# First attention of a fused two-layer kernel: values computed once per pair of token tiles, keys stored by even and odd chunk

## What is computed

```
x = x + attention(layernorm(x))          # 4 sequences of 1024 tokens, 256 features
qkv = xn @ W_qkv                         # 256 -> 3 x (16 heads x 16)
allowed = (j <= i) & (j > i - 64)        # each query sees itself and 63 tokens before it
out = softmax(q k^T / 4 + mask) v        # per head
return out @ W_out
```

## Time and profile before

| | |
|---|---|
| median of 3 runs | 2348.84 us |
| the profiled execution's own time | 2363.76 us |
| its span in the profile | 2362.0 us, mean granted clock 0.906 |
| first attention | 0 to about 460.8 us |
| matmuls of the values (L551), first attention | 384 |

### The profile page before, as it was taken

One profiled execution on the slowest core, in us unless ns is written; L12 is line 12 of the kernel. 1 busy time (PEld: TensorE's weight loads), 2 busy tenths in 40 slices (PEclk: granted clock), 3 DMA queues, 4 the chain that ended last, 5 costly groups with the idle time before them and its releaser, 6 DMA issues. The chain is left out here.

```text
span 2362.0 us, 49456 instructions
## 1 busy us (share of the span) xinstructions
PE 2011.9 (85%) x18325; PEld 1356.7 (57%) x18325; DVE 1704.1 (72%) x2695; ACT 1213.4 (51%) x2196; POOL 474.0 (20%) x610
## 2 busy tenths in 40 slices
PE   5889888799979999989978899999999999971270
PEld 4667666468879999978867333343343343330150
DVE  5666666566658888856644789999999999647822
ACT  4455454343256666632233278888888888530010
POOL 1010001010022322224343112112212211300054
PEclk9899999799989999999989589999999999675585
DMA  2000000191043333333268886854864701020054
GB/s 90 2 0 0 0 0 0 60 342 62 28 157 124 120 111 120 107 100 113 89 206 281 105 73 59 73 38 43 67 41 44 62 20 37 19 72 0 27 159 136
DMA packets 222809, 188.18 MB, mean 80 GB/s; under 512 B 121533, under 2 KB 201369, under 8 KB 220505
## 3 DMA queue, kind: packets, MB, share of 16 engines
q1 hardware_dynamic: 202872, 146.71, 30.9%
q0 software_dynamic: 18080, 27.17, 4.3%
q10 hardware_dynamic: 1728, 12.58, 1.5%
HBM read 121.37 MB, written 64.75 MB: 79 GB/s over the span
## 5 line engine op out<-in xcount | busy, mean ns | idle before, releaser
L2029 ACT ACTIVATE ga_probT<-banks 128x512 f32<-128x512 f32 x1024 | 556.7, 597 | 172.7 <-PE banks L2089 124.7
L1986 DVE TENSOR_REDUCE ga_nmax<-banks 128x1 fp32r<-128x1024 f32 x512 | 610.4, 1218 | 27.9 <-PE banks L2076 26.7
L2076 PE MATMUL banks<-a_ks,a_qs 48*128 48x512 f32 x1024 | 390.8, 465 | 9.5 <-PEq L77 5.7
L2089 PE MATMUL banks<-a_qs,a_ks 49*128 49x512 f32 x1024 | 390.1, 461 | 2.3 <-ACT ga_probT L2029 2.3
L2106 PE MATMUL banks<-ga_probT,a_v 128*32 128x256 f32 x4096 | 342.1, 408 | 6.2 <-ACT ga_o L2035 6.2
L2076 PEld LDWEIGHTS banks<-a_ks,a_qs 48*128 48x128 f32 x1024 | 158.9, 195 | 224.7 <-DVE ga_nmax L1986 171.5
L1952 POOL DMA_DIRECT2D a_qs<-ga_max_rows x256 | 130.8, 519 | 578.4 <-DVE ga_max_rows L1993 537.1
L1447 PE MATMUL banks<-rb_xT,rb_own_w 128*128 128x256 f32 x1872 | 232.1, 283 | 5.2 <-DVE rb_xT L1313 3.5
L1447 PEld LDWEIGHTS banks<-rb_xT,rb_own_w 128*128 128x128 f32 x1872 | 224.5, 190 | 11.5 <-issue 8.1
L2106 PEld LDWEIGHTS banks<-ga_probT,a_v 128*32 128x32 f32 x4096 | 82.9, 110 | 203.8 <-ACT ga_probT L2029 146.8
L1153 PE MATMUL banks<-m_xnT,sh_w 128*128 128x512 f32 x768 | 184.2, 398 | 6.6 <-DVE sh_w L942 5.3
(11 more groups left out here) (327 smaller groups left out, 3240.3 us busy)
## 6 DMA issues: line engine op xcount, KB each, us to landing
rb_w_f<-in_L_ffn_rw_dram SPq DMA_DIRECT2D x39, 512.0 KB
m_xnT<-xnT_parts ACTq DMA_DIRECT2D x12, 1024.0 KB, 4.8
sorted_out<-rb_yb SPq DMA_DIRECT2D x39, 256.0 KB, 2.1
m_w<-in_L_ffn_rw_dram SPq DMA_DIRECT2D x2, 4096.0 KB, 20.3
values<-pg_v SPq DMA_DIRECT2D x16, 512.0 KB, 3.1
a_v<-values SPq DMA_DIRECT2D x16, 512.0 KB, 8.8
a_qs<-queries_rounded SPq DMA_DIRECT2D x28, 256.0 KB, 8.6
a_ks<-keys_rounded SPq DMA_DIRECT2D x28, 256.0 KB, 10.4
```

The lines of the kernel that those rows point to most:

```text
L1986: nc.vector.tensor_reduce(nmax[b % 2][:, at:at + 1], slot[:], axis=AX.X, op=ALU.max, negate=True).then_inc(use_read, 1)
L2029: nc.scalar.activation(probT[k % SETS][2 * h + n][:], b_t[ring_place["weights", w] % RING][:], ACT.Exp, scale=SCALE).then_inc(exp_ready, 1)
L2076: return nc.tensor.matmul(slot[:, HALF * kh:HALF * (kh + 1)], qs[a][rows, n, P * q:P * (q + 1)], ks[a][rows, n, HALF * kh:HALF * (kh + 1)] ...
L2089: nc.tensor.matmul(bank[:], ks[a][rows, 2 * gp + n, P * kt:P * (kt + 1)], qs[a][rows, 2 * gp + n, HALF * hf:HALF * (hf + 1)], start=True, ...
```

## The change

1. `wa_xnT` loses its 64 tail columns, and ScalarE's two tail copies (L473) with the wait behind them go, as do two memsets.
2. Values are computed once: 12 matmuls per tile, at place 6, for the tile's two runs of 128 tokens. The use of `between` at place 5 goes, so each step has 6 uses of a bank in place of 7.
3. Even chunks are always on partitions 0 to 63 of a value block, odd chunks on 64 to 127. ScalarE writes them from the one bank in four instructions: blocks 1 and 3 whole (128x512), the even halves of blocks 0 and 2 (64x512), the odd half of block 2 (64x256), and the odd half of the *next* tile's block 0 (64x256, into the other buffer), the last behind a wait for the output products of the current tile's first half.
4. `wa_kT` becomes 8 slots of 64 columns: even chunks in slots 0 and 1, odd ones in 4 and 5, the previous tile's last chunk in slot 3. The key projection (L539) reads x in this order, and each score matmul (L584) reads its 128 key columns as two runs of 64, the even chunk first.
5. The masks of the first half of the queries are built with the two chunks exchanged.

```diff
-        xnT = [sb(f"xnT_{part}", [P, KD, WIN + 2 * P], F32R)
+        xnT = [sb(f"xnT_{part}", [P, KD, 2 * P], F32R)
-        kT = [sb(f"kT{a}", [P, KD, WIN + 2 * P]) for a in range(2)]
+        kT = [sb(f"kT{a}", [P, KD, 2 * KEYS, WIN]) for a in range(2)]
...
-            for part in xnT:
-                nc.gpsimd.memset(part[:, :, 0:WIN].bitcast(F32), 0.0)
-            nc.gpsimd.memset(kT[0][:, :, 0:WIN], 0.0).then_inc(tails_zero, 1)
+            nc.gpsimd.memset(kT[0][:, :, EARLIER], 0.0).then_inc(tails_zero, 1)
...
-                uses += [(1, "x", 1, 0), (2, "q", 1, 0), (4, "k", 1, 0), (5, "v", 1, 0), (6, "v", 1, 1)]
+                uses += [(1, "x", 1, 0), (2, "q", 1, 0), (4, "k", 1, 0), (6, "v", 1, 0)]
...
-                                act.wait_ge(v_done, ONE + 2 * i)
+                                act.wait_ge(v_done, ONE + i)
                                 act.wait_ge(x_rest, ONE + i)
-                                for part in xnT:
-                                    nc.scalar.activation(part[:, :, 0:WIN], part[:, :, 2 * P:2 * P + WIN].bitcast(F32),
-                                                         ACT.Copy).then_inc(x_tail, 1)
-                                act.wait_ge(x_tail, ONE + 2 * i)
...
-                            act.wait_ge(v_done, ONE + 2 * i + s + 1)
+                            new = bank[:].rearrange("p (a h d) -> p a h d", a=2, h=NH)
+                            act.wait_ge(v_done, ONE + i + 1)
                             if c + shift >= 2:
                                 act.wait_ge(out_done, ONE + UP * (i - 1))
-                            nc.scalar.activation(v[a][:, 2 * s:2 * s + 2, :, 0:DH],
-                                                 bank[:].rearrange("p (a h d) -> p a h d", a=2, h=NH),
-                                                 ACT.Copy).then_inc(v_ready, 1)
+                            nc.scalar.activation(v[a][:, 1:4:2, :, 0:DH], new, ACT.Copy).then_inc(v_ready, 1)
+                            nc.scalar.activation(v[a][half(0), 0:3:2, :, 0:DH], new[half(0)], ACT.Copy).then_inc(v_ready, 1)
+                            nc.scalar.activation(v[a][half(1), 2, :, 0:DH], new[half(1), 0], ACT.Copy).then_inc(v_ready, 1)
+                            if not first:
+                                act.wait_ge(out_done, ONE + UP * (i - 1) + NU)
+                            nc.scalar.activation(v[1 - a][half(1), 0, :, 0:DH], new[half(1), 1], ACT.Copy).then_inc(v_ready, 1)
...
                 elif kind == "v":
-                    if c + shift > 0:
-                        pe.wait_ge(x_tail, ONE + 2 * i)
                     for h in range(2):
-                        at = P * s + Q * h
+                        at = P * h
...
-                            last = nc.tensor.matmul(b_s[two][half(h), W2 * j:W2 * (j + 1)],
-                                                    q_heads[a][rows, j // HP, j % HP, at:at + Q], kT[a][rows, j // HP, at:at + P],
+                            keys = kT[a][rows, j // HP, s:s + EARLIER + h + 1:EARLIER + h, :]
+                            last = nc.tensor.matmul(b_s[two][half(h), W2 * j:W2 * (j + 1)].rearrange("p (a w) -> p a w", a=2),
+                                                    q_heads[a][rows, j // HP, j % HP, at:at + Q], keys,
                                                     start=False, stop=True, skip_group_check=True)
...
                 if m == 0:
-                    pe.wait_ge(v_ready, ONE + 2 * i + s + 1)
+                    pe.wait_ge(v_ready, ONE + 4 * i + 4)
```

More of the change, by code:

```diff
@@ L175, in window_attention @@
     HO = NU // 2
+    KEYS = 4
+    EARLIER, LATEST = KEYS - 1, KEYS + 1
     with phase(nc) as (e, semaphore, begin):
@@ L207, in window_attention @@
         consts_set, tails_zero, v_zero, v_set = sem("consts_set"), sem("tails_zero"), sem("v_zero"), sem("v_set")
-        xn_ready, xnT_done, xnT_ready, x_tail, k_tail = [sem(n) for n in (
-            "xn_ready", "xnT_done", "xnT_ready", "x_tail", "k_tail")]
+        xn_ready, xnT_done, xnT_ready, k_tail = [sem(n) for n in (
+            "xn_ready", "xnT_done", "xnT_ready", "k_tail")]
         q_copied = sem("q_copied")
@@ L244, in _ @@
             nc.gpsimd.memset(mask1[:], 0.0)
-            for part in xnT:
-                nc.gpsimd.memset(part[:, :, 0:WIN].bitcast(F32), 0.0)
-            nc.gpsimd.memset(kT[0][:, :, 0:WIN], 0.0).then_inc(tails_zero, 1)
+            nc.gpsimd.memset(kT[0][:, :, EARLIER], 0.0).then_inc(tails_zero, 1)
             link(nc.gpsimd.memset(head_rows[:], 1.0))
             for h in range(2):
[L251 to L255, removed]
+                m = mask1[half(h)].rearrange("p (a w) -> p a w", a=2)
+                chunk, base = (WIN, 0) if h else (-WIN, WIN)
+                link(nc.gpsimd.affine_select(out=m, in_=m, compare_op=ALU.is_ge, fill=NEG, base=WIN - base,
+                                             pattern=[[-chunk, 2], [-1, WIN]], channel_multiplier=1))
+                link(nc.gpsimd.affine_select(out=m, in_=m, compare_op=ALU.is_ge, fill=NEG, base=base - 1,
+                                             pattern=[[chunk, 2], [1, WIN]], channel_multiplier=-1))
             link(nc.gpsimd.tensor_copy(mask0[:], mask1[:].unsqueeze(1).broadcast_to([P, NP, W2])))
             m = mask0[half(0)].rearrange("p (b j) w -> p b j w", b=B)[:, :, 0, :]
-            nc.gpsimd.affine_select(out=m, in_=m, compare_op=ALU.is_ge, fill=NEG, base=-WIN,
-                                    pattern=[[0, B], [1, W2]], channel_multiplier=0)
+            nc.gpsimd.affine_select(out=m, in_=m, compare_op=ALU.is_ge, fill=NEG, base=WIN - 1,
+                                    pattern=[[0, B], [-1, W2]], channel_multiplier=0)
             for r in range(P // R):
@@ L489, in step @@
                                 act.wait_ge(k_ready, ONE + i)
-                                nc.scalar.activation(kT[a][:, :, 0:WIN], kT[1 - a][:, :, 2 * P:2 * P + WIN], ACT.Copy).then_inc(k_tail, 1)
-                            nc.scalar.activation(kT[a][:, :, WIN:WIN + 2 * P], bank[:].rearrange("p (k q) -> p k q", k=KD),
-                                                 ACT.Copy).then_inc(k_ready, 1)
+                                nc.scalar.activation(kT[a][:, :, EARLIER], kT[1 - a][:, :, LATEST], ACT.Copy).then_inc(k_tail, 1)
+                            nc.scalar.activation(kT[a][:].rearrange("p k (o f) w -> p k o (f w)", o=2)[:, :, :, 0:P],
+                                                 bank[:].rearrange("p (k o q) -> p k o q", k=KD, o=2), ACT.Copy).then_inc(k_ready, 1)
                         elif kind == "v":
-                            act.wait_ge(v_done, ONE + 2 * i + s + 1)
+                            new = bank[:].rearrange("p (a h d) -> p a h d", a=2, h=NH)
+                            act.wait_ge(v_done, ONE + i + 1)
                             if c + shift >= 2:
                                 act.wait_ge(out_done, ONE + UP * (i - 1))
-                            nc.scalar.activation(v[a][:, 2 * s:2 * s + 2, :, 0:DH],
-                                                 bank[:].rearrange("p (a h d) -> p a h d", a=2, h=NH),
-                                                 ACT.Copy).then_inc(v_ready, 1)
+                            nc.scalar.activation(v[a][:, 1:4:2, :, 0:DH], new, ACT.Copy).then_inc(v_ready, 1)
[4 more added lines that the diff above has]
+                            nc.scalar.activation(v[1 - a][half(1), 0, :, 0:DH], new[half(1), 1], ACT.Copy).then_inc(v_ready, 1)
             steps(act, step)
@@ L512, in bank_read @@
                  "k": lambda: pe.wait_ge(k_ready, ONE + i + 1),
-                 "v": lambda: pe.wait_ge(v_ready, ONE + 2 * i + s + 1),
+                 "v": lambda: pe.wait_ge(v_ready, ONE + 4 * i + 4),
                  "project": lambda: pe.wait_ge(x_ready, ONE + 2 * i + s + 1)}[kind]()
@@ L535, in use @@
                     part = ("q", "k").index(kind)
+                    order = ("p (o f w) -> p o f w", "p (f o w) -> p o f w")
                     for m in range(KD):
+                        dst = bank[:, 2 * P * m:2 * P * (m + 1)]
+                        if part:
+                            dst = dst.rearrange(order[0], o=2, w=WIN)
                         for k in range(KD):
                             for a, b in PASSES:
-                                last = nc.tensor.matmul(bank[:, 2 * P * m:2 * P * (m + 1)],
-                                                        w_parts[:, a, k, D * part + P * m:D * part + P * (m + 1)],
-                                                        xnT[b][:, k, WIN:WIN + 2 * P],
+                                src = xnT[b][:, k, :].rearrange(order[1], o=2, w=WIN) if part else xnT[b][:, k, :]
+                                last = nc.tensor.matmul(dst, w_parts[:, a, k, D * part + P * m:D * part + P * (m + 1)], src,
                                                         start=(k == 0 and a + b == 0), stop=(k == KD - 1 and a == 1))
```

6 lines of the change are left out of this document (3 added, 3 removed).

## The result

The changed kernel takes 2327.6 us, the median of 6 runs (2320.59 to 2331.07), against 2349.3 us for the kernel before in 6 runs of the same series. The medians differ by 21.7 us. The ratio of the two series is 0.9901, with a 95% interval of 0.9875 to 0.9926, which makes 23.3 us less, between 17 and 29. 2324.7 us was forecast, 24.1 less.

The account below looks back on a forecast made before the run. A chain alike in each first-attention tile was taken to bound, with PE binding at the place 5 value block and VectorE behind place 6's scores. Savings 22.4 + 1.4 + 0.3 = 24.1 us took 2348.84 to 2324.7 us, range 2312 to 2339.

Parts of the forecast that it names:

- The block at place 5: In tiles 2 to 15, removing this value block brings the scores and VectorE's maximum 1.6 us earlier: 22.4 us in all.
- The start: In tile 0, whose two value blocks run with nothing beside them, twelve fewer matmuls save 1.4 us.
- tile 1: In tile 1, most of the at most 1.0 us gained before the maximum is lost; 0.3 us saved.
- Copies, tails, constants at 0: ScalarE's four value copies at place 6 just fit; dropped tail copies at place 1 and fewer GpSimd memsets: each 0.
- Keys in two runs at 0: In first attention's score matmuls, reading the keys as 64 + 64 columns apart costs nothing: 0 us.
- The slower rival: Chance 0.05: key reads in two runs slow the scores; if doubled, they add 70.4 us, making 2395.1 us.
- The whole wait goes: Rival, chance 0.06: the maximum at place 6 gains all 2.27 us of VectorE's wait; 34.2 us saved, 2314.6 us.
- The clock: Rival, chance 0.06: PE's clock falls in each of 14 tiles; 11 more falls at 2.21 us cost 24.3: 2349.0 us.
- The sum: Over first attention, the terms 22.4, 1.4 and 0.3 us add up to 24.1 us saved.

Follow-up runs that it names:

- Experiments 1 and 2: Changed kernel with 12 unread value matmuls back at place 5: 2362.43 us beside 2356.53; kernel before without its place 5 value block and copy: 2303.03 beside 2327.91.
- experiment 6: The changed kernel and the kernel before, both run once more unedited: 2306.93 us against 2330.79 us, ratio 0.9895.
- experiment 4: Changed kernel with two more 128x512 ScalarE copies of the value bank, each waited for, ahead of the four: 2346.68 us beside 2356.53 for the kernel before.
- experiment 5: Changed kernel with its one remaining value block at place 5 in place of 6: 2380.16 us against 2356.53 for the kernel before, ratio 1.0124.

## Why the prediction was right

- **The block at place 5.** Right in place and mechanism, a little oversized: 1.42 us a tile, not 1.6. I had taken 1.6 between 1.43 and 1.71, because L610 in the earlier trace rows was held up by ScalarE:

```profile
427.89 0.29 PEld L610 LDWEIGHTS banks<-wa_probT,wa_v 128*32 128x32 f32 x16 [0.33 <-ACT wa_probT L449]
```

  It is held up so in the other tiles too, by the same 0.33 us: from projection to output products the changed kernel needs 0.96 us, as tile 15 did, to the hundredth. The lower bound was the answer, and 14 tiles give 19.9 us, not 22.4. Experiments 1 and 2 show that the block alone makes it.
- **The start.** 1.4 us was forecast, and by the first maximum the changed kernel was 2.16 us ahead (27.00 against 29.16 us): beside the 12 matmuls, the step between matmuls fell from 0.21 to 0.12 us at about 23.2 us, not at 24.6. The granted clock reads 1.00 there in both profiles, so that this is the clock is my reading. By the query heads of tile 2 (68.02 against 69.29) it was 1.27 ahead, with tile 1's share in it: 0.6 us of 30.46, where 0.3 was forecast. Of start and tile 1 together 1.7 was forecast. Tile 0 has a fall of the clock of 6.8 us where it had been 3.4. In the second pair of profiles (experiment 6), where it is so too, the two kernels are level at that point (68.91 and 68.90). So this term is worth between nothing and 1.3 us; no run separates it further.
- **Copies, tails, constants at 0.** Right: 24.1 us with tails put back and with two more copies. For the copies my reason was wrong: I set their end by durations against one exp and found 0.04 us, where the exp had 0.24 and the path at least 1.2 (experiment 4). The Trainium skill's figures for them (ScalarE: Activation LUTs, Rules for kernel authors), which it gives for an ACTIVATE whose bias is a pointer operand, as these copies' is not, would have made 6.6 us of loss out of a wait that PE doesn't feel. The trace has 598 and 367 to 380 ns beside the 0.72 and 0.51 us estimated from them. Neither these numbers nor mine should have been taken to the path without asking who waits for the exp.
- **Keys in two runs at 0.** Right: the scores take 1.10 us per 32 records, as in the earlier trace rows, and experiments 1 and 2 leave nothing over for them. The slower rival falls.
- **The whole wait goes.** Did not happen: VectorE still waits 0.84 us of the 2.27.
- **The clock.** The rival in which every tile has a fall was given 0.06, and in the changed kernel it didn't come. But its mechanism is real and its price was, if anything, low: with the one block at place 5 the clock fell in all 13, for 2.1 to 3.6 us each where 2.21 was reckoned. I had argued that the matmuls go from a stretch where PE never rests, and experiment 5 bears that out: had the change kept the block at place 5 and dropped the one at 6, it would have made the kernel slower by 1.2%.
- **The sum.** 24.1 us, against 21.7 by the medians and 23.3 by the ratio; with 1.42 a tile it would have been 21.6, inside the interval as well. The time of 2327.6 us lies in the range of 2312 to 2339. What the tiles show is 19.9 us, plus 0 to 1.3 for the start. The other 1 to 3 us are within what the clock moves, so that 24.1 lies as near to the ratio's 23.3 as it does is in part luck.

## What to carry to other kernels

When one of two equal blocks of PE work can go, find which of them stands where PE bounds, and keep the one that stands where PE would wait: here it cost nothing there and kept the clock up. Cost the kept block's place as well as the removed one's, and read slack at the engine that waits last, not at the first instruction that comes late. Measure small gains by the length of the repeated tile, since the 1.9 ms that nobody touched moved by up to 45 us from profile to profile.

## What was not expected of the hardware

- Moving 12 matmuls by one place, with no change in their number, took the mean clock over 13 tiles from 0.99 and 0.97 to 0.85 and the kernel from 0.99 to 1.01 of the time before. In the tile looked at, both waits that preceded the fall were short, 1.22 and 1.13 us.
- Matmuls whose results nobody reads may be worth something: 72 of them in tiles 1 and 15, and 84 more in the others, go with the version of the lowest median, and with shorter falls or none in those two tiles.
